# A transformer layer with a mixture of experts: the maxima products of an attention head dealt out four to a period over four periods, and one set of products with ones issued a period earlier

## The reference, cut to what matters

```python
attn = jnp.einsum('bnd,bmd->bnm', q * scale, k)                 # 12 heads, 1024 x 1024 scores each
attn = add_decomposed_rel_pos(attn, q, rel_pos_h, rel_pos_w, (h, w), (h, w))
attn = jax.nn.softmax(attn.astype(jnp.float32), axis=-1).astype(q.dtype)
out = attn @ v                                                  # 1024 x 32 per head
...
x = x + conv(ln(x));  t = t + moe(ln(t))                        # moe: router, top 2 of 8 experts, 384 -> 1536 -> 384
```

## Time and profile before

| | |
|---|---|
| median of 3 runs | 649.78 us (648.08 to 650.61) |
| profiled execution | 647.42 us, of which the span from first to last instruction is 645.6 us |
| TensorE's mean granted clock | 0.984 of full speed |
| PE busy, share of the span | 94% |
| DVE, ACT, POOL busy | 61%, 47%, 27% |
| attention, one head of the loop | 19.24 us |

### The profile page before, as it was taken

One profiled execution on the slowest core, in us unless ns is written; L12 is line 12 of the kernel. 1 busy time (PEld: TensorE's weight loads), 2 busy tenths in 40 slices (PEclk: granted clock), 3 DMA queues, 4 the chain that ended last, 5 costly groups with the idle time before them and its releaser, 6 DMA issues.

```text
span 645.6 us, 11986 instructions
## 1 busy us (share of the span) xinstructions
PE 608.9 (94%) x4473; PEld 505.7 (78%) x4473; DVE 394.6 (61%) x664; ACT 300.7 (47%) x419; POOL 172.0 (27%) x106
## 2 busy tenths in 40 slices
PE   3998999999999999999976999999999999999996
PEld 3876866665656655656865899999999999999994
DVE  7567676556566566662478887547654675557635
ACT  4654335444444444446164544444543554354523
POOL 1300076556775555776600000000000000000000
PEclk9999999999999999999986999999999999999998
DMA  8045054442234443100250442434444433443302
GB/s 263 2 82 124 1 123 83 83 84 58 45 60 81 81 81 65 54 0 2 99 183 1 129 160 83 165 125 151 144 147 147 146 119 118 149 164 110 111 1 98
DMA packets 37410, 63.33 MB, mean 98 GB/s; under 512 B 3864, under 2 KB 32894, under 8 KB 37246
## 3 DMA queue, kind: packets, MB, share of 16 engines
q1 hardware_dynamic: 37374, 62.83, 34.6%
HBM read 44.16 MB, written 1.57 MB: 71 GB/s over the span
## 4 chain that ended last, share of the span: by engine, by line
PE 84%; DVE 9%; ACT 2%; POOL 2%; issue 1%; DMA 1%; SPq 1%; POOLq 0%; DVEq 0%
PE ps L747 20%; PE ps L763 20%; PE ps L551 11%; PE ps L560 9%; PE ps L537 8%; PE ps L461 6%; DVE rhalf L1113 5%; POOL acc L395 2%; PE ps L491 1%; PE ps L718 1%; PE ps L773 1%; PE ps L581 1%; DMA onehot<-c_onehot 1%; PE ps L446 1%; PE ps L780 1%
## 5 line engine op out<-in xcount | busy, mean ns | idle before, releaser
L1113 DVE TENSOR_REDUCE rhalf<-ps 128x1 f32<-128x512 f32 x192 | 128.6, 689 | 62.8 <-PE ps L537 62.6
L906 ACT ACTIVATE prob<-ps 128x1024 f32<-128x1024 f32 x96 | 96.8, 1026 | 106.8 <-PE ps L551 106.8
L395 POOL TENSOR_TENSOR acc<-acc,prob 128x1024 f32<-128x1024 f32 x48 | 115.3, 2403 | 6.0 <-ACT prob L906 2.1
L551 PE MATMUL ps<-qst,kst 128*128 128x512 f32 x384 | 108.6, 397 | 0.0
L747 PE MATMUL ps<-xeh,wih 128*128 128x320 f32 (+1 forms) x288 | 89.9, 312 | 1.0 <-ACT xeh L968 1.0
L537 PE MATMUL ps<-kst,qst 128*128 128x512 f32 x192 | 84.2, 442 | 7.0 <-DVE rhalf L1113 3.2
L763 PE MATMUL ps<-hh,woh 128*128 128x320 f32 x288 | 89.4, 310 | 0.0
L763 PE MATMUL ps<-hl,woh 128*128 128x320 f32 x288 | 89.2, 310 | 0.0
L747 PE MATMUL ps<-xel,wih 128*128 128x320 f32 (+1 forms) x288 | 89.2, 310 | 0.0
L747 PE MATMUL ps<-xeh,wil 128*128 128x320 f32 (+1 forms) x288 | 89.1, 309 | 0.0
L763 PE MATMUL ps<-hh,wol 128*128 128x320 f32 x288 | 89.1, 309 | 0.0
(11 more groups left out here) (157 smaller groups left out, 927.3 us busy)
## 6 DMA issues: line engine op xcount, KB each, us to landing
raw_i<-in_L_ffn_wi SPq DMA_DIRECT2D x32, 576.0 KB, 4.9
raw_o<-in_L_ffn_wo SPq DMA_DIRECT2D x32, 576.0 KB, 4.0
xs<-in_x SPq DMA_DIRECT2D x8, 384.0 KB, 4.6
qst<-qh SPq DMA_DIRECT2D x12, 256.0 KB, 3.1
qst<-relh SPq DMA_DIRECT2D x12, 256.0 KB, 3.9
qst<-relw SPq DMA_DIRECT2D x12, 256.0 KB, 4.5
kst<-kp SPq DMA_DIRECT2D x12, 256.0 KB, 5.2
qst<-ql SPq DMA_DIRECT2D x12, 128.0 KB, 3.1
```

The lines of the kernel that those rows point to most:

```text
L395: nc.gpsimd.tensor_tensor(acc[:, :], acc[:, :], prob[:, t % SLOT, :], ALU.add).then_inc(sum_add, 1)
L551: last = mm(bank(2 * (t % 2) + half), kst[b][:, part, t * P:(t + 1) * P], qst[b][:, part, half * BANK:(half + 1) * BANK], start=part == 0, ...
L906: run(prob[:, t % SLOT, :], ps[:, 2 * (t % 2) * BANK:2 * (t % 2 + 1) * BANK], ACT.Exp).then_inc(exp_done, 1)
L1113: ve.tensor_reduce(rhalf[:, p // 2, p % 2:p % 2 + 1], bank(4 + p % 2), AX_X, ALU.max).then_inc(max_red, 1)
```

## The change

Every head's 16 maxima products are made in four lots of four instead of five, five and six. Products 4 to 15 of head h + 1 lie in periods 0, 1 and 2 of head h, and period 3 takes products 0 to 3 of head h + 2. Head 0 makes all 16 of head 1 as before and then the first four of head 2. Head 10 makes only 4 to 15 of head 11. VectorE's order follows: 12 reductions of head h + 1, `whole_max`, `negate_max`, then 4 reductions of head h + 2; `normalise(h - 1)` stands ahead of reduction 12, in period 2, where it stood ahead of reduction 10. The products with ones of tile 6 are issued with `values(h, b, 2)`, behind a wait for that tile's exponential, and not with `values(h, b, 3)`. SP's, ScalarE's and GpSimd's programs are the same.

```diff
+                if i == PAIRS_T - 2:
+                    pe.wait_ge(exp_done, NT * h + ADDED + 1)
+                    last = quarters(slice(Q4, 2 * Q4), ones[:, 0:HD], prob[:, ADDED % SLOT, :], False, False)
                 if i == PAIRS_T - 1:
-                    for t in range(ADDED, NT):
+                    for t in range(ADDED + 1, NT):
                         quarters(slice(Q4, 2 * Q4), ones[:, 0:HD], prob[:, t % SLOT, :], False, False)
...
-            PIECES = [(0, 5), (5, 10), (10, 16), (16, 16)]
+            FIRST_PIECES = [(0, 5), (5, 10), (10, 16)]
-            def head(h, n, b, first=False, last=False):
+            def head(h, n, b, first=False, last=False, more=True):
-                nxt = (n + b // 2, (b + 1) % 3)
+                nxt = (h + 1, n + (b + 1) // 3, (b + 1) % 3)
+                after = (h + 2, n + (b + 2) // 3, (b + 2) % 3)
                 def maxima(pieces):
-                    for p in pieces:
-                        max_scores(h + 1, *nxt, p)
+                    for head_max, p in pieces:
+                        max_scores(*head_max, p)
                 for i in range(PAIRS_T):
-                    pieces = [] if last else list(range(*PIECES[i]))
+                    if last:
+                        pieces = []
+                    elif i == PAIRS_T - 1:
+                        pieces = [(after, p) for p in range(4)] if more else []
+                    elif first:
+                        pieces = [(nxt, p) for p in range(*FIRST_PIECES[i])]
+                    else:
+                        pieces = [(nxt, p) for p in range(4 * i + 4, 4 * i + 8)]
...
-            head(NH - 2, (NH - 2) // 3, (NH - 2) % 3)
+            head(NH - 2, (NH - 2) // 3, (NH - 2) % 3, more=False)
...
-            def head(h, first=False):
-                for p in range(2 * NT):
-                    if p == 10 and not first:
+            def head(h, first=False, more=True):
+                for p in range(0 if first else 4, 2 * NT):
+                    if p == 12 and not first:
                         normalise(h - 1)
                     reduce_max(h + 1, p)
                 whole_max(h + 1)
                 negate_max(h + 1)
+                if more:
+                    for p in range(4):
+                        reduce_max(h + 2, p)
...
-            with dve.Fori(1, NH - 1) as h:
+            with dve.Fori(1, NH - 2) as h:
                 head(h)
+            head(NH - 2, more=False)
```

## The result

The changed kernel takes 633.92 us (median of 4 runs, 632.73 to 634.5) against 649.76. The ratio is 0.9759, with a 95% interval of 0.9741 to 0.9777. The prediction was 634.9.

A forecast was written before the change was run, and what follows sets the result against it. PE was taken to bound the kernel, stalled by DVE's reductions of maxima: 1.49 us a head over 10 heads gives 14.9, all other parts 0, so 649.78 - 14.9 = 634.9 us; range 631 to 643.

The forecast's parts named there:

- The bound and the price of a late reduction: Attention stage: PE bounds; maxima products wait for reductions, stalling 0.34, 0.34 and 0.81 us in periods 0 to 2.
- Ten heads times 1.49: Heads 1 to 10 lose all three stalls, 1.49 us each, 14.9 us in all; likeliest case, chance 0.78.
- The turn of the maxima: PE's turn after the last reduction: cost 0, margin 0.05 us; rival up to 0.70 a head, 641.9, chance 0.09.
- Uncovered drains: Rival: tiling switches at three value blocks a head, formerly covered by stalls, cost 0.27 each, 8.1 us, 643.0; chance 0.05.
- the row at 174.54: Value block behind eight streamed scores also takes 1.00 us, so a switch behind busy PE was costed at 0.
- The operands: Head h + 2's operands, wanted a fourth of a head earlier: cost 0; slower rival, too late, 656, chance 0.04.
- For head 2: Operands at head 0's end: DMA engines quiet from 93 us, L543 at 95.4, so cost 0.
- The set of ones: Four products of tile 6, 0.25 us, move from period 1 to period 0, no wait for the exponential: cost 0.
- GpSimd before head 11: GpSimd's additions of head 11: 3.1 of 4.92 us idle time remain, so the gain reaches the end whole.

The follow-up runs named there:

- The experiment with the seventh tile: Changed kernel with GpSimd adding up seven tiles instead of six in heads 0 to 10: 630.73 us, ratio 0.9721.
- the relief of head 0: Changed kernel with products 0 to 7 of head 1 made behind head 0's value tiles: 634.52 us, ratio 0.9771.
- one fifth piece: Changed kernel with one maxima product moved back into period 0 (five, three, four) in heads 1 to 10: 639.6 us, ratio 0.9823.

## Why the prediction was right

**The bound and the price of a late reduction** stand. The stall of 0.34 us was given back alone and measured 0.34 in the chain and 0.36 by the pace. The three stalls, 1.49 us a head, are the whole difference of 19.24 and 17.75. That only the fifth and sixth piece stall is shown by the empty list of waits on L1124.

**Ten heads times 1.49.** 14.9 predicted; 192.4 - 177.5 = 14.9 in the profiles; 15.8 between the medians. The interval of the ratio times 649.78 is 633.0 to 635.3, which holds 634.9. That the median came within 1.0 us of the forecast is in part luck: medians of the same changed kernel lay at 633.92 and 634.85.

**The turn of the maxima.** No new wait: L543 follows the values in the chain. The product behind it takes 0.30 or 0.31 us in seven of the ten heads and 0.41 or 0.42 in three. The scores that stood there before had the first part of this as well: eight of them took 1.92 where a stream takes 1.85. Only the 0.1 in three heads is new, 0.03 a head that I had at nothing.

**Uncovered drains.** The value blocks still take 1.00 us behind an unstalled product, in all periods. The rival is out, and the row at 174.54 in the earlier trace rows had said so. A switch does have a price: a product in a stream takes 0.23 and the first one directly behind a block of values 0.43, before the change and after it, so 0.20 us. It is paid behind a busy array as behind a stalled one. The Trainium skill, in TensorEngine Tiling, section Key Properties, says that changing the tiling mode drains TensorE. These rows do not contradict that; whether the 0.20 us are such a drain, no run here shows.

**The operands.** Right for the loop, and the experiments bracket the threshold: 4.4 us later is free, 9.2 later makes the kernel 4% slower. One step of the working was off without showing: I had product 0 at 171.1, 15.8 us behind the release at 155.3, and it came 15.1 behind it, since three of the products that leave the first three periods (0.69) had stood in that stretch and I had not taken them off. The gather takes 8.6 us to land, somewhat more than the 8 read from the DMA share. My price for this rival, the gather plus 2.9 a head, counted the waiting alone; the lower clock behind each wait nearly doubled it. For head 2 I wrote off the matter with 2.4 us to spare, counted to the fall of the DMA share and not to the landing. It was enough, and too little for the next step.

**The set of ones.** It was mis-sized: 0.43 us, not 0.25. I took the 16 records of a value block for 16 products. By the program a block is 8 products of 256 columns, four a tile, and the profile shows each as two records. A set of ones is 4 products, the one with `acc` no more than that of a tile, and so 8 records (24 against 16 in the row of 1.43). As the term was moved and not removed, the sum didn't feel it. The experiment with the seventh tile did.

**GpSimd before head 11.** 3.1 us of idle time were to remain, and 3.02 did:

```profile
282.94 2.42 POOL L391 TENSOR_TENSOR acc<-prob 128x1024 f32<-128x1024 f32 x1 [3.02 <-PE ps L560]
```

## What to carry to other kernels

Where a fast engine hands work to a slower one through two buffers, the spacing decides, not the count: give each piece other work between it and its next but one, and let the last piece of a group stand ahead of a long block. Read the price of such a stall from the chain, as the time between the two products less the work that lies between them; the waits of the weight loads, here 20.3 us in 9.9 heads, overstate it by more than a third. And when a stall goes, look up what has the least cover next, at the edges of the pipeline too: here it was the operands of head 2, and the relief of head 0 ended there.

## What the runs showed of the hardware

- PE's granted clock fell after idle stretches of some 2.8 us, and not always in the same way. In the kernel with the gather held back by four tiles it was 0.50 from 141 to 147 us behind one wait and from 165 to 167 behind the next. Behind the third, which ended at 186.99, the first four score products still took 0.93 us, and the clock was 0.50 from 189 to 191. The heads with these waits took 23.7, 22.2 and 22.2 us against 17.75. On the mean of nine heads a wait of 2.8 us cost 4.8.
- The spread of the runs is in the stretch between attention and experts. From the last turn to the first product of the experts (`xeh`) it was 71.1 us in the first profile of the changed kernel, 72.7 in the second and 72.8 in that with one fifth piece; from there to the end it was 286.5, 286.4 and 286.9. In that stretch PE stops and starts, and the granted clock between 300 and 350 us was 0.83, 0.80 and 0.76. The mean over the span was 0.986, 0.983 and 0.978. This spread bounds what a median of few runs can tell: the pace in the profile told 0.1 us a head apart, the medians about 2 us.
- The release that the profile names can be another than the real one: behind the scores of tile 6, ScalarE's exponential at 151.93 in the changed kernel is put down to GpSimd's addition, yet the scores ended at 151.74, 0.19 before it, the same gap as in other tiles, and the program waits there for an addition that was long done.
